# MetaFormer block on one core: the involution's projection made once per row, its two x neighbours copied inside SBUF

## The reference, cut to what matters

```python
x = x + conv(ln_c(x))                      # ln_c: mean and variance over the 128 channels
t = t + ffn(ln_t(t))                       # graph attention, top 2 of 4 experts

def conv(x):
    r  = relu(batch_norm(x @ Wr + br))                 # 128 -> 32
    w  = (r @ Ws + bs).reshape(B, H, W, 16, 1, 9)      # 9 weights for each of 16 groups
    xi = x @ Wi + bi                                   # the projection, 128 -> 128
    xp = pad(xi, one position on each side in y and x)
    patches = stack([xp[:, i:i+H, j:j+W, :] for i in range(3) for j in range(3)], axis=3)
    patches = patches.reshape(B, H, W, 16, 8, 9)       # the 9*128 numbers, cut in another way
    return sum(w * patches, axis=-1)
```

## Time and profile before

| | us |
|---|---|
| median of three runs (2842.95 to 2855.72) | 2843.73 |
| the profiled execution | 2834.66 |
| its span, first to last instruction | 2832.8 |
| the first step of the conv stage on DVE starts | 37.10 |
| the last step starts | 501.28 |

### The profile page before, as it was taken

One profiled execution on the slowest core, in us unless ns is written; L12 is line 12 of the kernel. 1 busy time (PEld: TensorE's weight loads), 2 busy tenths in 40 slices (PEclk: granted clock), 3 DMA queues, 4 the chain that ended last, 5 costly groups with the idle time before them and its releaser, 6 DMA issues.

```text
span 2832.8 us, 22266 instructions
## 1 busy us (share of the span) xinstructions
PE 1002.3 (35%) x4867; PEld 675.7 (24%) x4867; DVE 2124.0 (75%) x4081; ACT 780.2 (28%) x1624; POOL 1202.6 (42%) x1234
## 2 busy tenths in 40 slices
PE   6778777499922110099543322350000000000000
PEld 3455445266611110066322221230000000000000
DVE  5989999999789992999488888875633412822888
ACT  3555555244411110044332222221000000000344
POOL 0000000000000005777777764777777777736750
PEclk8766777699955555599775666675555555555555
DMA  2222324992200002133231212124212113342676
GB/s 62 67 67 71 82 70 178 393 138 74 74 15 0 0 0 27 25 83 82 61 47 35 43 37 40 39 46 41 36 20 24 20 10 24 46 42 82 188 240 226
DMA packets 259502, 202.29 MB, mean 71 GB/s; under 512 B 101592, under 2 KB 207445, under 8 KB 258902
## 3 DMA queue, kind: packets, MB, share of 16 engines
q1 hardware_dynamic: 189766, 114.21, 17.2%
q0 software_dynamic: 46336, 44.61, 8.8%
q10 hardware_dynamic: 23314, 42.60, 4.7%
HBM read 94.51 MB, written 107.07 MB: 71 GB/s over the span
## 4 chain that ended last, share of the span: by engine, by line
DVE 28%; PE 21%; POOL 18%; DVEq 14%; issue 10%; ACT 5%; DMA 3%; ACTq 1%; SPq 0%; POOLq 0%
POOL sb_rows_g L782 16%; PE bank L1022 7%; DVE sb_xi L1678 7%; PE bank L1012 6%; DVEq L1694 5%; DVE sb_xi L1685 3%; DVE sb_inv L1383 2%; PE bank L938 2%; DVE sb_hid_y L1518 2%; DVEq L1414 2%; PE bank L1001 2%; DVEq L1404 2%; DVE sb_y_new L2172 1%; PE bank L1019 1%; DVE sb_new L1907 1%
## 5 line engine op out<-in xcount | busy, mean ns | idle before, releaser
L782 POOL DMA_INDIRECT sb_rows_g<-scr_node,sb_srcs x1024 | 1001.4, 978 | 312.1 <-issue 311.7
L1685 DVE TENSOR_TENSOR sb_xi<-sb_xi 128x512 f32<-128x512 f32 (+2 forms) x852 | 427.2, 568 | 46.7 <-ACT sb_xi L1171 33.0
L1001 PE MATMUL bank<-sb_ident,sb_xi 128*128 128x128 f32 x448 | 99.5, 410 | 532.6 <-DVE sb_xi L1685 280.3
L1678 DVE TENSOR_TENSOR sb_xi<-sb_xi 128x1024 f32<-128x1024 f32 (+2 forms) x258 | 243.5, 944 | 27.5 <-ACT sb_xi L1176 8.7
L1022 PE MATMUL bank<-sb_w,sb_hid_y 128*128 128x128 f32 x2048 | 262.6, 281 | 0.0
L782 POOL DMA_INDIRECT sb_hid_y<-scr_level,sb_row_at x8 | 7.9, 985 | 597.3 <-DVE sb_row_at L1442 595.1
L1012 PE MATMUL bank<-sb_tnT_in,sb_w 128*128 128x512 f32 x512 | 238.5, 618 | 57.7 <-DVE sb_sinks L1790 33.5
L1679 DVE TENSOR_TENSOR sb_xi<-sb_xi 128x1024 f32<-128x1024 f32 (+2 forms) x258 | 245.7, 952 | 0.0
L1022 PEld LDWEIGHTS bank<-sb_w,sb_hid_y 128*128 128x128 f32 x2048 | 238.2, 191 | 29.0 <-issue 29.0
L1194 ACT ACTIVATE sb_hid_y<-bank,sb_b1c 128x512 f32<-128x512 f32 x256 | 163.6, 691 | 233.4 <-PE bank L1012 231.5
L1001 PEld LDWEIGHTS bank<-sb_ident,sb_xi 128*128 128x128 f32 x448 | 85.6, 216 | 545.0 <-DVE sb_xi L1685 286.8
(11 more groups left out here) (340 smaller groups left out, 2127.0 us busy)
## 6 DMA issues: line engine op xcount, KB each, us to landing
scr_expert_out<-sb_y_new ACTq DMA_DIRECT2D x64, 512.0 KB, 3.8
sb_y_in<-scr_expert_out SPq DMA_DIRECT2D x32, 1024.0 KB, 6.7
scr_state<-sb_zeros POOLq DMA_DIRECT2D x6, 4096.0 KB, 55.5
sb_rows_g<-scr_node,sb_srcs POOLq DMA_INDIRECT x1024
scr_state<-sb_state SPq DMA_DIRECT2D x16, 768.0 KB, 6.4
scr_tnT<-sb_tnT SPq DMA_DIRECT2D x34, 256.0 KB, 2.0
sb_tnT_in<-scr_tnT ACTq DMA_DIRECT2D x34, 256.0 KB, 2.7
sb_xa<-in_x SPq DMA_DIRECT2D x64, 128.0 KB, 2.5
```

Of the source, the lines that this page charges most:

```text
L782: pool.indirect_dma_start(to, None, table, bass.IndirectOffsetOnAxis(ap=index, axis=0), **kw).then_inc(s, 16)
L1001: last = pe.transpose(bank[b][:, m * P:(m + 1) * P], src[:, (4 * b + m) * P:(4 * b + m + 1) * P], ident[:, :])
L1678: dve.tensor_tensor(vb[:, :, 0], va[:, :, 0], va[:, :, 1], ALU.min)
L1685: last = dve.tensor_tensor(vb[:, :, d, :, c], va[:, :, d, :, 0], va[:, :, d, :, 1], ALU.min if c == d else ALU.max)
```

## The change

PE makes the projection of a row once. `conv_products` has one bias matmul of 512 columns for four rows (ones times the three bf16 parts of the bias) and four products, one per row, in one bank; they come ahead of the product by `wr`. ACT copies the four rows with one instruction to block j = 1. SP then copies, within SBUF, block 1 of partitions 0 to 125 to block 0 of partitions 2 to 127, and block 1 of partitions 2 to 127 to block 2 of partitions 0 to 125 (`shift_rows`): two transfers of 126 partitions x 4 rows x 512 bytes for each chunk, issued in SP's step i for chunk i+2 behind the two loads of `sb_xa`. POOL writes zeros once at the image's edges. DVE's step i waits for the copies of chunks i and i+1. The masks `valid` and `valid9` and the padded columns are gone.

At the start, DVE takes the first statistics before it makes its constants, and ACT's first instructions follow. Some semaphores are merged.

```diff
         def conv_products(i, u):
             pe.wait_ge(xnT_ready, i + 1)
+            if some(i - 1):
+                pe.wait_ge(xi_ready, i - 1)
+            po = bank[4 + u]
+            pe.matmul(po[:, :].rearrange("p (r f) -> p r f", f=C), ones[:, :], over(bi_rows[:, :], ROWS),
+                      start=TR, stop=FA)
+            for r in range(ROWS):
+                last = pe.matmul(po[:, r * C:(r + 1) * C], xnT[:, u, r], wi[:, :], start=FA, stop=r == ROWS - 1)
+            last.then_inc(xi_psum, 1)
             if some(i):
                 pe.wait_ge(rT_ready, i)
-            pe.matmul(bank[1][0:CR, :], wr[:, :], xnT[:, u, :, 2:P + 2],
+            pe.matmul(bank[1][0:CR, :], wr[:, :], xnT[:, u, :, :],
                       start=TR, stop=TR).then_inc(r_psum, 1)
-            for r in range(ROWS):
-                po = bank[4 + r % 2]
-                if some(ROWS * i + r - 1):
-                    pe.wait_ge(xi_ready, ROWS * i + r - 1)
-                pe.matmul(po[:, 0:3 * C], valid9[:, :], bi9[:, :], start=TR, stop=FA)
-                for j in range(3):
-                    last = pe.matmul(po[:, j * C:(j + 1) * C], xnT[:, u, r, 2 * j:2 * j + P], wi[:, :],
-                                     start=FA, stop=j == 2)
-                last.then_inc(xi_psum, 1)
...
         def conv_copies(q, c, u):                      # ACT
+            act.activation(xi_rows[:, shifted_rows(c), 1], bank[4 + u][:, :].rearrange("p (r f) -> p r f", f=C),
+                           ACT.Copy).then_inc(xi_ready, 1)
...
+        def shift_rows(i, c, u):                       # SP
+            y = shifted_rows(c)
+            sp.wait_ge(xi_ready, i + 1)
+            put(xi_rows[2:P, y, 0], xi_rows[0:P - 2, y, 1], xi_shifted[u])
+            put(xi_rows[0:P - 2, y, 2], xi_rows[2:P, y, 1], xi_shifted[u])
...
             if more(i, 4):
                 sp.wait_ge(normed1, i + 3)
                 load_xa(*after(q, c, 4), u)
+            if more(i, 2):
+                shift_rows(i + 2, after(q, c, 2)[1], u)
             sp.wait_ge(conv_done, i + 1)
...
-            dve.wait_ge(xi_ready, ROWS * (i + 1) + (1 if more(i, 1) else 0))
+            if not begin:                              # every step but step 0
+                dve.wait_ge(xi_shifted[u], 32 * (turn + 1))
+                if more(i, 1):
+                    dve.wait_ge(xi_shifted[1 - u], 32 * (turn + u + 1))
             dve.wait_ge(w_ready, i + 1)
```

More of the change, by code:

```diff
@@ L440, in params, with shifted_rows @@
             ]
-        def bias_params():
-            return [(bi3[j:j + 1, j * C:(j + 1) * C], bi.unsqueeze(0)) for j in range(3)]
+        def shifted_rows(c):
+            return ds(ROWS * c + 1, ROWS)
         def late_params():
@@ L569, in _ @@
                 load_xa(0, 2 + u, u)
+            for u in (0, 1):
+                sp.wait_ge(xi_bordered, 2)
+                shift_rows(u, u, u)
+            sp.wait_ge(xi_bordered, 4)
             with nc.allow_non_contiguous_dma(reason="columns of a few numbers"):
@@ L756, in _ @@
                           channel_multiplier=P).then_inc(consts_made, 1)
-            pool.memset(zeros[:, :], 0.0).then_inc(zeros_made, 1)
+            pool.memset(zeros[:, :], 0.0).then_inc(consts_made, 1)
             pool.iota(nearest_i[:, :], pattern=[[1, NEAR]], base=0, channel_multiplier=0).then_inc(consts_made, 1)
-            pool.wait_ge(ident_zero, 3)
+            pool.wait_ge(ident_zero, 1)
             pool.affine_select(out=ident[:, :], in_=ident[:, :], compare_op=ALU.not_equal, fill=1.0,
                                base=0, pattern=[[-1, P]], channel_multiplier=1).then_inc(consts_made, 1)
[L763 to L773, removed]
+            pool.wait_ge(consts_made, CONSTS)
+            for n, (first, end) in enumerate(((1, 2 * ROWS + 1), (2 * ROWS + 1, NY + 1))):
+                if n:
+                    pool.wait_ge(xi_bordered, 2 * n)
+                pool.memset(xi_rows[0:2, first:end, 0], 0.0).then_inc(xi_bordered, 1)
+                pool.wait_ge(xi_bordered, 2 * n + 1)
+                pool.memset(xi_rows[P - 32:P, first:end, 2], 0.0).then_inc(xi_bordered, 1)
+            pool.wait_ge(consts_made, CONSTS)
+            pool.wait_ge(edges_loaded, 32)
             for flat in (starts_d, state_d):
@@ L958, in node_products @@
             def node_products(i, u):
+                if not some(i):
+                    pe.wait_ge(bn_ready, 4)
                 pe.wait_ge(tnT_ready, i + 1)
@@ L1297, in _ @@
             flush = dve.drain
-            dve.wait_ge(consts_made, CONSTS)
-            dve.tensor_copy(nearest[:, :], nearest_i[:, :])
-            for k in range(LOG_E - LOG_C):
-                dve.tensor_scalar(sign_i[:, k:k + 1], part[:, :], k, 1,
-                                  ALU.logical_shift_right, ALU.bitwise_and)
-            dve.tensor_copy(partf[:, :], part[:, :])
-            for k, v in enumerate((1e-6, 1e-5, 1e-3)):
-                dve.memset(eps[:, k:k + 1], v)
-            dve.memset(zero[:, :], 0.0)
@@ new lines, in _ @@
+            dve.wait_ge(bias_loaded, 16)
+            left = bi_whole
+            for k in range(3):
+                dve.tensor_copy(bi_parts[:, k], left).then_inc(bias_split, 1)
+                flush()
+                if k == 0:
+                    first_scales(0)
+                if k < 2:
+                    dve.tensor_tensor(bi_left, left, bi_parts[:, k], ALU.subtract)
+                    left = bi_left
+                    flush()
+            dve.memset(xi[:, 0:3 * C], 0.0)
+            dve.memset(rT[CR:CR + 1], 1.0).then_inc(bn_ready, 1)
@@ new lines, in _ @@
+            first_scales(1)
+            first_sums(2)
+            dve.wait_ge(params_loaded, 16 * len(params()))
+            for k in (0, 1):
+                dve.tensor_tensor(prod[:, k * HE:(k + 1) * HE], att[:, k], wgat[:, 0:HE], ALU.mult)
+            flush()
+            for k in (0, 1):
+                dve.tensor_reduce(wgat[:, HE + k * HEADS:HE + (k + 1) * HEADS],
+                                  prod[:, k * HE:(k + 1) * HE].rearrange("p (h e) -> p h e", e=EXPERTS), AX.X,
+                                  ALU.add).then_inc(bn_ready, 1)
@@ new lines, in _ @@
+            dve.memset(xi[:, (NY + 1) * 3 * C:], 0.0)
+            dve.wait_ge(consts_made, CONSTS)
+            dve.tensor_copy(nearest[:, :], nearest_i[:, :])
+            for k in range(LOG_E - LOG_C):
+                dve.tensor_scalar(sign_i[:, k:k + 1], part[:, :], k, 1,
+                                  ALU.logical_shift_right, ALU.bitwise_and)
+            dve.tensor_copy(partf[:, :], part[:, :])
+            dve.memset(zero[:, :], 0.0)
+            dve.memset(most[:, :], float(EDGES))
@@ L1373, in products @@
+            dve.memset(keyb[:, 0, 0:1], 0)
+            for k in (0, 1):
+                dve.tensor_scalar(target[:, k], target[:, k], SRC_BITS, None, ALU.logical_shift_left)
+                dve.tensor_scalar(edge_target[:, k], edge_target[:, k], SRC_BITS, None, ALU.logical_shift_left)
+            flush()
+            dve.tensor_scalar(signs[:, :], sign_i[:, :], -2.0, 1.0, ALU.mult, ALU.add).then_inc(small_ready, 1)
+            first_scales(2)
             def products(c, u, r):
@@ L1399, in conv_step @@
                 reduction(0)
+                row_there(1)
                 products(c, u, 1)
```

171 lines of the change are left out of this document (71 added, 100 removed).

## The result

| | before | changed |
|---|---|---|
| median, us | 2843.34 (4 runs, 2832.26 to 2855.72) | 2878.75 (4 runs, 2876.44 to 2880.86) |
| the profiled execution, us | 2834.66 | 2880.86 |
| ratio to before | | 1.012 (95% interval 1.0083 to 1.0158) |

The changed kernel is 1.2% slower. The forecast was 14.4 us slower than before, 2858.1 in all; measured are 35.4 between the medians and 46.2 between the two profiled executions (that of before lies near the low end of its runs). The direction was right, the size was off by more than a factor of two, and the time lies above the range.

What follows compares the result with a forecast made beforehand. DVE was taken to bound the steady conv step, PE and ACT only where DVE waits. Won 10.9 + 13.0 = 23.9, lost 8 + 6.9 + 9.4 + 14 = 38.3: net 14.4 us slower, 2858.1, range 2834 to 2875.

Steps and rivals of the forecast that it cites:

- The start: Start of the conv stage: step 1 begins near 40.4 instead of 51.27, a gain of 10.9 us, between 7 and 14.
- waits for ACT's root: DVE's waits for ACT's square root in the conv stage: 13.0 of the 13.9 us won, through less PE work.
- copies in loop steps: 22 loop steps: copies land 0.6 us late in one step of two, 0.15 in the other; 8 us lost.
- node stores: Step 19: chunk 20's copies, behind the `sb_xa` loads pushed back by the node stores, land near 335; 6.9 us lost.
- edge lists: Step 29: chunk 30's copies queue behind the edge lists and land near 484.3; 9.4 us lost, between 7.5 and 11.
- stores of zeros: Step 30: chunk 31's copies pass under POOL's stores of zeros and land near 511.5; 14 us lost, between 8 and 19.
- Rival 2: SP bounds the loop: with issues of 1.1 us, 26 us are lost instead of 8, time 2876; chance 0.15.
- The 1.6 us that the rule added: Copies under the stores of zeros: 126 partitions over 14 engines, 1008 pieces need 12.8 instead of 11.2 us; left outside the sum.
- Rival 1: Copies don't stand in line in the queue: none of the four losses, 23.9 us won, time 2820; chance 0.13.
- Rival 3: PE falls to half clock for good, having less to do; the 13.0 us come back as waits: 2871; chance 0.10.

Runs made afterwards that it cites:

- experiment 1: The changed kernel with DVE's wait for the copies of chunk i+1 moved from the step's start to ahead of its fourth row: 2838.35 us, ratio 0.9949 to before.
- experiment 3: The changed kernel with SP issuing the two copies of chunk i+2 ahead of the two `sb_xa` loads: 2861.91 us, ratio 1.0045 to before.
- experiment 5: The changed kernel with one copy per chunk, the right neighbour's left out and block 2 zero: 2847.17 us, ratio 0.997 to before.
- experiment 2: The changed kernel with POOL's two long memsets of the edges of `sb_xi` waiting until DVE's three bias casts are done: 2877.29 us, ratio 1.0094 to before.
- experiment 4: The changed kernel with POOL's seven stores of zeros waiting for the copies of all chunks: 2866.88 us, ratio 1.0059 to before.
- experiment 6: The changed kernel with node stores issued behind step 17's copies and edge lists behind the last chunk's copies: 2849.36 us, ratio 1.0016 to before.

## Why the prediction was right in direction and wrong in size

| term of the sum | predicted | measured | error |
|---|---|---|---|
| the start | -10.9 | -1.3 | +9.6 |
| waits for ACT's root | -13.0 | -13.5 | -0.5 |
| copies in loop steps | +8 | +22.5 | +14.5 |
| node stores | +6.9 | +7.6 | +0.7 |
| edge lists | +9.4 | +9.7 | +0.3 |
| stores of zeros | +14 | +19.0 | +5.0 |
| step 30 and all behind step 31 | 0 | +2.1 | +2.1 |
| sum | +14.4 | +46.1 | |

**The copies in loop steps**, the step that failed most: a term of 8 us that measured 22.5. The mechanism was as described (experiments 1, 3 and 5); the size was wrong. The same step of the changed kernel, step 22, starting at 380.47, answers to the earlier trace rows:

```profile
389.76 1.45 SPq L520 DMA_DIRECT2D sb_xa<-in_x  x2
...
391.50 2.13 SPq L520 DMA_DIRECT2D sb_xi<-sb_xi  x2
...
394.49 0.38 DVE L1313 BATCH_NORM_AGGREGATE sb_mv<-sb_stats 128x2 f32<-128x6 f32 x4
...
396.62 1.36 DVE L1394 TENSOR_TENSOR sb_prod<-sb_xi,sb_wv 128x1152 f32<-128x1152 f32 x1 [1.75 <-DMA sb_xi<-sb_xi]
```

The prediction put the copies 11.15 us into the step; they are issued at 11.03. It had the second land at 15.15 and took that as the start of the next step. The second copy is issued 12.18 into it, 0.13 later than assumed. It lands 3.65 us after that, by its last semaphore update at 396.30 (the measure of the earlier trace rows), where the sum had 2.4 and 0.7. That is the largest of the errors: a single copy takes 3.4 us in experiment 5, against 2.4 to 2.5 for a load, and the sum gave it the time of a load and 0.7 for being the second. Another 0.32 passes until the product starts at 396.62, behind two more waits. And without a wait DVE's step now takes 14.40, not 14.55, so it comes 0.15 earlier to the wait. These four, 0.13 + 0.55 + 0.32 + 0.15, make 0.6 into 1.75. The steps to which I gave half a microsecond more room, 0.15 late, wait 1.1 to 1.4 (0.4 of it stood there before the change): their copies are issued only 0.4 earlier. There was no slack left to hide any of this, so each error of a few tenths counted in full, in some 20 steps. Rival 2 gave nearly the right loss, 26, and almost the right time, 2876; a part of its reason is true, as one copy takes 0.99 us to issue and the next begins 1.15 behind it, where I had assumed 0.65 to 0.9. That SP as a whole bounds the loop, its wording, is refuted by experiment 1, so its number came near by luck.

**The start.** ACT's root of the first statistics is at 8.55, as predicted (8.4). The prediction then had DVE free; it was in a cast until 11.10. POOL's memsets were booked at nothing, without a word in the working, because nobody waits for them at that point. What they share with DVE was not asked. The predicted copy at 13 is at 20.55 in the changed kernel, and at 13.2 in experiment 2, which brings back 6.7 of the missing 9.6 us (step 1 at 43.3 where the prediction had 40.4). The second half of the term, that step 1 waits for chunk 2 and gives back a part, was right: 4.6 us of wait here, 4.2 in experiment 2.

**The stores of zeros.** The wait was predicted at 14 and is 18.5. The step starts at 499.90, and q1's pieces flow from 9.5 us into it, where the prediction had 8.2. The 1648 pieces then take 22 us, 75 per us instead of 90; the prediction had 18.3 (and 492.5 and 18.3 make 510.8, not its 511.5). The loads' last completion is at 518.3, that of the copies at 531.5, 13.2 us later, where I had 11.2, and 12.8 by the rule of the Trainium skill ("DMA: Bandwidth & Descriptors", "Why a DMA increments its semaphore by 16 and not by 1"). The trace agrees with that rule: each copy ends with 14 completion packets, each load with 16. The pace fits too, as an estimate from the packet records: in the 6.35 us before 518.3 the queue passes 534 pieces, nearly all of the loads (84 per us); in the 13.2 us behind it 1045, of which by count 971 are the copies' (74 per us) and the others belong to the next stores, beside them. 74 to 84 is 14 to 16. The 1.6 us that the rule added should have been in the sum.

**Right**: the roots' waits (13.5 of 13.9 gone, and gone in experiment 1 as well, so the late copies don't hide them), the node stores and the edge lists, each within 0.7 us. The last two were worked out from where the copies stand in SP's order. Experiments 4 and 6 show that these waits come from what is ahead of the copies: moved, they go, all but the 3.3 us at step 19. Rival 1 (pieces overtake) is refuted by the same runs. Rival 3 is too: PE's granted clock fell, from 0.76 of full to 0.54 between 333 and 476 us, and no long wait for ACT's root came back.

## What to carry to other kernels

Where a change adds a transfer to a pipeline, ask at which instruction its data is needed and put the wait there: one wait moved by 9 us was worth 1.7% here, 49 us, against 13.5 us of waits that PE's smaller work removed. Don't give a new kind of transfer the landing time of another one (3.4 us for a copy, 2.5 for a load), count on to the start of the consumer, and where a transfer is expected within a microsecond of its use in a step that repeats, work out what each tenth more would cost. And an instruction off the critical path is free only if the engines share nothing with it.

## What the runs showed of the hardware

- A cast of 128 numbers in one partition on DVE takes 0.15 to 0.21 us, and 5.3 to 5.4 under a 6.06 us memset on POOL, ending 0.1 behind it. Seven shifts of 128 x 1 integers are held up in the same way (3.25 instead of 0.50); memsets, statistics and operations on two tensors are not (experiment 2).
- A copy within SBUF of 126 partitions x 4 x 512 bytes lands 3.4 us after its issue begins (experiment 5), the second of a pair 3.5 to 3.7 in the loops of the changed kernel, against 2.4 to 2.5 for a load from HBM of half as many pieces (the earlier trace rows and the changed kernel). Its issue takes 0.94 to 0.99 us, against 0.60 to 0.65. Staying inside SBUF made neither short; whether the number of pieces or the target makes the difference, no run shows.
- A transfer of 126 partitions ends in 14 completions, one of 64 x 4 pieces in 16; under the stores of zeros the pieces of the first pass at about 74 per us, those of the second at 84.
